# A four-layer graph kernel on one core: bias rows written by ScalarE, and a new order of VectorE's and ScalarE's work in the node stretches

## What is computed

```
H  = concat(x, A x, A A x, A A A x) @ W0 + b0        # A: weighted sum over the edges
x1 = layernorm(x + H)
h  = relu(concat(x1, sum/max/mean of edge features, u) @ W1 + b1)
x2 = layernorm(x1 + h @ W2 + b2 + x1)
x3 = layernorm(x2 + attention(q[dst], k[src], v[src]) + x2 @ Ws + bs)
x4 = layernorm(x3 + (x3 + 3 * A' x3) / 4)
```

## Time and profile before

| | us |
|---|---|
| median of 3 runs | 6894.02 (6891.36 to 6906.69) |
| the profiled execution | 6887.08 |
| its span | 6885.1 |
| PE busy | 4858.4 (71%) |
| DVE busy | 4473.3 (65%) |
| POOL busy | 4340.7 (63%) |
| ACT busy | 2790.1 (41%) |

### The profile page before, as it was taken

One profiled execution on the slowest core, in us unless ns is written; L12 is line 12 of the kernel. 1 busy time (PEld: TensorE's weight loads), 2 busy tenths in 40 slices (PEclk: granted clock), 3 DMA queues, 4 the chain that ended last, 5 costly groups with the idle time before them and its releaser, 6 DMA issues. The chain is left out here.

```text
span 6885.1 us, 103113 instructions
## 1 busy us (share of the span) xinstructions
PE 4858.4 (71%) x26012; PEld 3279.8 (48%) x26012; DVE 4473.3 (65%) x8278; ACT 2790.1 (41%) x5782; POOL 4340.7 (63%) x4335
## 2 busy tenths in 40 slices
PE   0068799999888799999989999978788870321110
PEld 0045566666566577777764444444444440221100
DVE  8855477777688688888853333349999991754420
ACT  0034455555455444444432222238888880110000
POOL 0067766664477477666646666647777762677777
PEclk9999999999999899999999999998888875555555
DMA  0022366666588689888865455443444439533321
GB/s 22 5 71 83 87 195 197 195 195 197 187 273 271 202 248 255 251 251 252 251 175 162 155 160 162 156 125 115 116 115 114 115 102 314 163 109 93 93 61 38
DMA packets 899323, 1090.55 MB, mean 158 GB/s; under 512 B 137109, under 2 KB 543521, under 8 KB 895492
## 3 DMA queue, kind: packets, MB, share of 16 engines
q1 hardware_dynamic: 757158, 816.08, 38.9%
q0 software_dynamic: 137984, 221.55, 12.5%
q10 hardware_dynamic: 4032, 51.38, 2.1%
HBM read 652.84 MB, written 497.99 MB: 167 GB/s over the span
## 5 line engine op out<-in xcount | busy, mean ns | idle before, releaser
L968 PE MATMUL bank<-ident,gat 128*128 128x128 f32 x2352 | 432.3, 313 | 807.6 <-DVE zT L1897 737.2
L1242 ACT ACTIVATE mbuf<-t 128x512 f32<-128x512 f32 x490 | 308.9, 630 | 1532.3 <-DVE t L1931 745.8
L1080 PE MATMUL bank<-W2s,hT 128*128 128x128 f32 x6272 | 817.4, 284 | 0.0
L1080 PEld LDWEIGHTS bank<-W2s,hT 128*128 128x128 f32 x6272 | 742.0, 194 | 89.8 <-issue 89.8
L1064 PE MATMUL bank<-x1T,W1x 128*128 128x512 f32 x1568 | 773.7, 606 | 9.2 <-ACT x1T L1232 5.1
L968 PEld LDWEIGHTS bank<-ident,gat 128*128 128x128 f32 x2352 | 295.7, 161 | 962.3 <-issue 769.8
L749 POOL DMA_INDIRECT pays<-PAY,s_q x392 | 379.9, 969 | 489.3 <-DVE s_v L1763 340.3
L968 PE MATMUL bank<-ident,x 128*128 128x128 f32 x3136 | 496.0, 281 | 206.0 <-DVE x L1864 189.5
L723 POOL DMA_INDIRECT gat<-X,d_x x392 | 393.8, 1005 | 329.2 <-issue 264.3
L1313 ACT ACTIVATE hT<-bank,b1u 128x512 f32<-128x512 f32 x784 | 496.2, 686 | 241.8 <-PE bank L1067 237.1
L968 PEld LDWEIGHTS bank<-ident,x 128*128 128x128 f32 x3136 | 356.0, 142 | 452.6 <-DVE x L1864 391.8
(11 more groups left out here) (359 smaller groups left out, 11556.8 us busy)
## 6 DMA issues: line engine op xcount, KB each, us to landing
X<-x SPq DMA_DIRECT2D x588, 256.0 KB, 3.0
fB<-row_s_same SPq DMA_DIRECT2D x392, 256.0 KB, 5.0
Y<-x SPq DMA_DIRECT2D x294, 256.0 KB
xT<-in_x_fm SPq DMA_DIRECT2D x196, 256.0 KB, 4.9
ffB<-rows_last_notlast SPq DMA_DIRECT2D x98, 512.0 KB
out_rows<-Y ACTq DMA_DIRECT2D x28, 1792.0 KB, 59.0
Z1T<-zT SPq DMA_DIRECT2D x98, 256.0 KB, 2.1
Z1E<-zE SPq DMA_DIRECT2D x98, 256.0 KB
```

What stands on the lines that cost most here:

```text
L968: mm = pe.transpose(dst[:, t, :], tiles[t], ident[:, :])
L1080: mm = pe.matmul(bMLP[:, t, :], hT[h][s][:, t * P:(t + 1) * P], W2s[:, h, :], start=False, stop=h == HC - 1, skip_group_check=True)
L1242: act.activation(sq[k % 3][s % 2], [bT1, t2[s], bSK, t2[s]][k][:, :, :], ACT.Square).then_inc(S(f"squared{k}", s), 1)
```

## The change

Three things are changed.

- **Bias rows.** At the start PE writes the two bias banks once with the bf16 matmul. ScalarE copies one row block of each to SBUF (`seed_a`, `seed_c`). From then on ScalarE copies that block, repeated four times, into the bank before each group (`seed_mm1` after the ln1 norm of the group before, `seed_mlp` after the `layer2` of the group before). PE waits for the copy and accumulates onto it. The 686 bias matmuls of the node stretches, s and d are gone; those of the attention stretch stay.
- **Order in the node stretches.** VectorE does norm ln2 in the same step as the sum it needs (lag 2, after both sums), not at the head of the next (lag 3). The scan of the z groups moves ahead of norm ln1, the weighing behind `layer2`. ScalarE's list begins with the seed and the squares of ln2 and ln3 (lags 3 and 4), and has square ln1 and the relu behind them. PE's, POOL's and SyncE's lists of stages are unchanged.
- **Order in s and d.** ScalarE's lists get the seeds, and nothing else moves. The semaphore `sums0` is merged into `carry0`.

```diff
--- before.py
+++ after.py
@@ -168,6 +168,7 @@
         bres2 = sb("bres2", [1, 3, P])
         bsp = sb("bsp", [1, 3, 3, P], BF16)
         bias3 = sb("bias3", [3, 3, P], BF16)
+        seed_a, seed_c = sb("seed_a", [P, P]), sb("seed_c", [P, P])
 
 
         s_q, s_src, s_v, s_out, d_x1, d_out = (sb(n, [P, EC], I32) for n in (
@@ -962,6 +963,11 @@
             pe.wait_ge(S("ld_bias"), 48)
             pe.wait_ge(S("consts"), 1)
 
+            for k, dst in enumerate((bT1, bMLP)):
+                mm = pe.matmul(dst[:, :, :], ones3[:, :], bias3[:, k:k + 1, :].to_broadcast([3, T, P]),
+                               start=True, stop=True, skip_group_check=True)
+            mm.then_inc(S("u_part"), 1)
+
             def turn(dst, tiles):
 
                 for t in range(T):
@@ -1007,14 +1013,13 @@
                 c = ci(kind, i)
                 if kind != "node" and void(pe, i, s, ("mm1", c, 1)):
                     return
-                prior(pe, "ln1_out", s, c)
+                ready(pe, "seeded_a", s, c)
                 if kind == "s":
                     ready(pe, "x_src", s, i)
                     ready(pe, "ld_z", s, i, 32)
                     ready(pe, "scanned", s, seq(2, i))
                 else:
                     ready(pe, "ld_x", s, i, 16)
-                bias(bT1, 0)
                 for t in range(T):
                     mm = pe.matmul(bT1[:, t, :], xT[s][:, t, :], W0I[:, 0, :], start=False,
                                    stop=kind == "node", skip_group_check=True)
@@ -1073,8 +1078,7 @@
                 if kind != "node" and void(pe, i, s, ("mlp", c, 1)):
                     return
                 ready(pe, "relu", s, c)
-                prior(pe, "t2", s, c)
-                bias(bMLP, 1)
+                ready(pe, "seeded_c", s, c)
                 for t in range(T):
                     for h in range(HC):
                         mm = pe.matmul(bMLP[:, t, :], hT[h][s][:, t * P:(t + 1) * P], W2s[:, h, :], start=False,
@@ -1228,6 +1232,28 @@
             act.wait_ge(S("b1u"), 1)
             act.wait_ge(S("consts"), 1)
 
+            act.wait_ge(S("u_part"), 2)
+            act.copy(seed_a[:, :], bT1[:, 0, :])
+            act.copy(seed_c[:, :], bMLP[:, 0, :]).then_inc(S("b1u"), 1)
+            act.wait_ge(S("b1u"), 2)
+
+            def seed(kind, name, bank_, row, freed, first=0):
+
+                def stage(i, s):
+                    c = ci(kind, i + first)
+                    if kind != "node" and void(act, i, s, (name, c, 1)):
+                        return
+                    prior(act, freed, s, c)
+                    act.copy(bank_[:, :, :], row[:, :].rearrange("p (o f) -> p o f", o=1).to_broadcast([P, T, P])
+                             ).then_inc(S(name, s), 1)
+                return stage
+
+            def seed_mm1(kind, first=0):
+                return seed(kind, "seeded_a", bT1, seed_a, "ln1_out", first)
+
+            def seed_mlp(kind, first=0):
+                return seed(kind, "seeded_c", bMLP, seed_c, "t2", first)
+
             def evac(dst, src, sem):
                 act.copy(dst, src).then_inc(sem, 1)
 
@@ -1325,14 +1351,15 @@
                 return stage
 
             def node(first):
-                return ((square("node", 0, first), 0), (std("node", 0, first), 0), (x2_out("node", first), 3),
-                        (relu("node", first), 1), (square("node", 1, first), 2), (std("node", 1, first), 2),
-                        (x1_out("node", first), 0), (square("node", 2, first), 3), (std("node", 2, first), 3))
+                return ((seed_mm1("node", first), 0), (square("node", 1, first), 3), (square("node", 2, first), 4),
+                        (std("node", 1, first), 3), (x1_out("node", first), 1), (std("node", 2, first), 4),
+                        (square("node", 0, first), 0), (seed_mlp("node", first), 2), (std("node", 0, first), 0),
+                        (relu("node", first), 1), (x2_out("node", first), 3))
 
             steps(act, N0, *node(0))
-            steps(act, EI, *node(N0)[:2], (z_rows(0), 4), *node(N0)[2:], peeled=1)
-            steps(act, N2, (half(z_rows(1), 1), 4), *node(N0 + EI)[:2], (half(z_rows(1), 0), 3), *node(N0 + EI)[2:],
-                  peeled=1)
+            steps(act, EI, *node(N0)[:6], (z_rows(0), 4), *node(N0)[6:], peeled=1)
+            steps(act, N2, *node(N0 + EI)[:6], (half(z_rows(1), 1), 4), *node(N0 + EI)[6:9],
+                  (half(z_rows(1), 0), 3), *node(N0 + EI)[9:], peeled=1)
             all_slots(act, "st_z2", 2 * EI * 16)
 
             def x_src(i, s):
@@ -1342,11 +1369,12 @@
                 reuse(act, "mm1", s, ci("s", i))
                 evac(xT[s][:, :, :], bBK[:, :, :], S("x_src", s))
 
-            steps(act, EI, (square("s", 0), 1), (std("s", 0), 1), (relu("s"), 2), (x2_out("s"), 4), (x_src, 0),
-                  (square("s", 1), 3), (std("s", 1), 3), (x1_out("s"), 1), (square("s", 2), 4),
+            steps(act, EI, (square("s", 0), 1), (std("s", 0), 1), (relu("s"), 2), (seed_mm1("s"), 0), (x2_out("s"), 4),
+                  (x_src, 0), (square("s", 1), 3), (seed_mlp("s"), 2), (std("s", 1), 3), (x1_out("s"), 1), (square("s", 2), 4),
                   (std("s", 2), 4), peeled=1)
 
-            steps(act, EI, (x1_out("d"), 0), (square("d", 1), 2), (std("d", 1), 2), (relu("d"), 1), peeled=1)
+            steps(act, EI, (x1_out("d"), 0), (square("d", 1), 2), (seed_mlp("d"), 1), (std("d", 1), 2), (relu("d"), 1),
+                  peeled=1)
 
             def att_src(i, s):
                 if void(act, i, s, ("att_src", i, 1)):
@@ -1941,18 +1969,18 @@
                 return norm(kind, 1, lambda s: t2[s], x2, "ln2_out", x2_free(kind), first)
 
             def node(first):
-                return ((norm2("node", first), 3), (power("node", 0, first), 0), (norm1("node", first), 0),
-                        (layer2("node", first), 2), (power("node", 1, first), 2), (power("node", 2, first), 3),
+                return ((power("node", 0, first), 0), (norm1("node", first), 0), (layer2("node", first), 2),
+                        (power("node", 1, first), 2), (power("node", 2, first), 3), (norm2("node", first), 2),
                         (norm("node", 2, lambda s: bSK, x4s, "ln4_out", x4_free, first), 3))
 
             steps(dve, N0, *node(0))
             for parity in range(2):
                 paid(dve, PB0, parity)
-            n2, p0, n1, l2, p1, p2, n3 = node(N0)
-            steps(dve, EI, n2, p0, n1, (z_weigh(0), 1), l2, p1, (z_scan(0), 2), p2, n3, peeled=1)
-            n2, p0, n1, l2, p1, p2, n3 = node(N0 + EI)
-            steps(dve, N2, n2, p0, n1, (half(z_scan(1), 0), 2), (half(z_weigh(1), 0), 1), l2, p1,
-                  (half(z_scan(1), 1), 2), (half(z_weigh(1), 1), 1), p2, n3, peeled=1)
+            p0, n1, l2, p1, p2, n2, n3 = node(N0)
+            steps(dve, EI, p0, (z_scan(0), 2), n1, l2, (z_weigh(0), 1), p1, p2, n2, n3, peeled=1)
+            p0, n1, l2, p1, p2, n2, n3 = node(N0 + EI)
+            steps(dve, N2, p0, (half(z_scan(1), 0), 2), n1, l2, (half(z_weigh(1), 0), 1), p1, p2,
+                  (half(z_scan(1), 1), 2), n2, (half(z_weigh(1), 1), 1), n3, peeled=1)
 
             all_slots(dve, "st_x1_", NI * 16)
             all_slots(dve, "st_x4", NI * 16)
@@ -2112,15 +2140,15 @@
             all_slots(dve, "hidden", NI + 2 * EI)
             dve.memset(den[SL - 1][:, :], 0.0)
             dve.memset(mbuf[SL - 1][:, :], 0.0)
-            dve.memset(agg[SL - 1][:, :], 0.0).then_inc(S("sums0"), 1)
-            dve.wait_ge(S("sums0"), 1)
+            dve.memset(agg[SL - 1][:, :], 0.0).then_inc(S("carry0"), 1)
+            dve.wait_ge(S("carry0"), 3)
 
             steps(dve, EI, (att_max, 1), (scale34, 4), (att_weigh, 2), (att_scores, 0), (att_sum, 2), (att_out, 3), peeled=1)
 
 
             all_slots(dve, "agg_turned", EI)
-            dve.memset(zT[SL - 1][:, :], 0.0).then_inc(S("sums0"), 1)
-            dve.wait_ge(S("sums0"), 2)
+            dve.memset(zT[SL - 1][:, :], 0.0).then_inc(S("carry0"), 1)
+            dve.wait_ge(S("carry0"), 4)
 
             def fin_scale(i, s):
                 if void(dve, i, s, ("fin_scaled", i, 1)):
```

## The result

The changed kernel takes **6601.01 us** (median of 4 runs, 6597.59 to 6607.28) where the kernel before took 6899.85 beside it (4 runs, 6891.36 to 6906.69): ratio 0.9571, 95% interval 0.9559 to 0.9583. The profiled execution has a span of 6605.4 us where before had 6885.1.

The account below looks back on a forecast made before the run. No engine full: POOL bounds stretch 1, a three-engine loop stretches 2 and 3 (POOL close in 3), VectorE s, the bias's relu wait d. -120 + 0 - 27 - 29 - 30 = -206 from 6887.1, plus 6.9: 6688 us; range 6650 to 6775.

Parts of the forecast that it names:

- The walk: One step of the second node stretch followed through the engines in the new order; nothing late, 8.06 us, 8.10 with jitter.
- The lower price of 0.22: The skill's formula for an isolated 512-column bias matmul, 0.22 us instead of 0.31; the time would be near 6724.
- POOL as the next bound: Second node stretch: POOL needs 7.8 us a step while loads last, 0.3 us away from PE's step.
- The bound of -130: Second node stretch's largest gain: POOL as the floor with PE below it, -130 us, against -120 forecast.
- Stretch 1: First node stretch, 44 groups: POOL's table loads and codes hold it, so 0 us, at best -7, at worst +3.
- Stretch 3: Third node stretch, 52 groups: gathers' part -18 us down to POOL's pace, draining steps -9, together -27 (0 to -35).
- s: Source stretch, 98 groups: VectorE's row bounds it; its 0.30 us wait for second-layer matmuls goes, -29 us (0 to -40).
- d: Destination stretch, 98 groups: relu lets the real matmul start at once, 0.31 us each, -30 us (0 to -35).
- B: Shorter gain: hand-overs delay ScalarE's x1T copy, second node stretch near 8.7 us a step, third keeps 10.5; 6766 us; chance 0.17.
- C: Source stretch: seeds cost what the bias gave (x2T or scan late), 29 us less gain, 6717 us; chance 0.12.
- D: Node stretches: the reorder does nothing, only one bias per step in the loop counts; -90 us, 6804 us; chance 0.05.
- E: Node stretches slower: ScalarE's queue becomes the loop, steps of 10.3 and 11.5 us; +90 us, 6984 us; chance 0.04.

Follow-up runs that it names:

- the experiment with the codes moved: Changed kernel with 1 code scatter per table block in the first node stretch instead of 3, the 86 codes moved to the destination stretch: 6504.61 us, ratio 0.9430.

## Why the prediction was right or wrong

**The step that failed** is "nothing is late, so PE runs unbroken: 9.30 - 0.62 wait - 2 x 0.31 = 8.06". The walk behind it was right: TensorE does run unbroken, but for the pauses that POOL makes. Both terms of the subtraction were too small. The wait was 0.96: the idle time in brackets counts from the modelled end of the matmul before, and start to start the hidden matmuls to x2's turn took 2.43 to 2.50 where an unbroken TensorE has 1.72. That is 0.71 to 0.78; the other 0.2 lies in three gaps without a bracket, x2's turn to the bias (0.59 for 0.53), layer 1 to the next turn (1.06 to 1.15 for 1.00) and that turn to the hidden matmuls (0.47 to 0.49 for 0.43). The biases were 2 x 0.51: I took the spacing from the bias to the next matmul and not what it did to the spacing ahead of it and behind the fp32 group. 9.30 - 0.96 - 1.03 = 7.31. The lower price of 0.22 that the prediction sets beside it would have been further off.

**POOL as the next bound** was named rightly (7.8 a step; 7.6 measured), but as one that TensorE's 8.06 would hide and for all 100 groups. It became the bound of the 86 that have loads; the others, and the draining steps, go at 7.31. With 100 groups and about two steps of draining, 86 x 7.6 + 16 x 7.3 = 770 of the 777.8. The bound of -130 in the range was therefore wrong too, and the range with it. It doesn't even follow from its own numbers: a floor of 7.8 against 9.30 is 1.5 us a step, or -150; with that in its place the range would have begun at 6630, still 29 us too high.

**Stretch 1** is right: 0 forecast, +0.8 measured, VectorE's last norm there begins at 732 and POOL ends the stretch; the experiment with the codes moved shows that POOL alone did. That it also did before the change is true by 5 us only.

**Seeds** of 0.59 to 0.60 us on average (0.6 assumed), costing nothing: right.

**Stretch 3**: the gathers' part fell by 18.6 us (18 forecast), at POOL's pace. The drain fell by 16 where I had 9. The undersized step explains a part (five steps 2.0 us shorter are 10); the rest isn't traced.

**s**: -37.6 against -29. With the bias off TensorE the stretch takes 1137 to 1140 us whatever the order in the node stretches and with or without seeds. My reason, VectorE's row, holds: the step fell from 11.73 to 11.32, and of these 0.41 us, 0.31 lie where I had put 0.30, between VectorE's scan and its addition (start to start 1.49 before, 1.18 after); the rest I didn't foresee. Nor did I see that POOL's eight gathers, lengthened by VectorE's own work, stood only 0.3 us behind as the next bound. **d**: -29.9 against -30; there TensorE waits for ScalarE's relu, 0.77 us before and after, and the real matmul starts at once, so the 0.31 from bias to matmul was the whole saving. The price of 0.31 that failed in stretch 2 was the right one here.

**The rivals**: B's hand-overs cost nothing measurable; C's wait came and was off the path; D falls with the order alone (-107 in stretch 2); E stayed away here; with the seed two places later its kind of loop appeared, at 0.16 us a step, and the lowered clock behind it cost more. Order and bias need each other: alone -107 and -1 in stretch 2, together -182.5.

## What to carry to other kernels

Price a removed instruction by start-to-start times ahead of it, over it and behind it, in a stretch where the engine is not waiting, and read a wait as the step less the same step unbroken; idle time in brackets after matmuls understated it here, 0.62 for 0.96. When a step shortens, compare each other engine's floor with the new step group by group; an engine without waits may still only be running ahead, and whether its consumer falls further behind from group to group tells. A prefill that moves to another engine is free only at the right place of that engine's queue. At the head of ScalarE's step the seed cost nothing; in the old order, ahead of the x1T copy, it took back the 51 us of stretch 2 that the missing bias gives; two places later it cost 123 us more, most of it by TensorE's clock.

## What the runs showed of the hardware

- A 512-column bf16 matmul of 3 rows between fp32 matmuls took 0.51 us of TensorE's time, its like directly behind it 0.22.
- ScalarE wrote a 128x512 fp32 bank in PSUM from a repeated 128x128 block in SBUF in 0.59 to 0.60 us on average (585 seeds).
- Waits of 1.91 us of TensorE, one a step, were followed in 38 of 90 steps by its lower clock (granted 0.50 from 1222 to 1224 us), and such a step took 11.20 us in place of 9.54.
- POOL's indirect gathers took 0.95 us, and up to 1.87 in s; the long ones lie beside VectorE's instructions with two SBUF operands, and shortening two such scans cut the mean of the x gathers from 1.06 to 0.946. The Trainium skill (GPSIMD Engine Reference, "Key points") says that GpSimd shares its SBUF interfaces with VectorE and contends with instructions that have two SBUF inputs; the trace agrees. What exactly is blocked during a gather, no run here shows.
